# Attention with relative positions on one core: the order in which sixteen products of the relative-value table are issued

## The chip, the core and the metric

The kernel runs on one core of a Trainium2 chip. The core has a matrix engine (TensorE, called PE in the profile, with its weight loads shown apart as PEld), VectorE (DVE), ScalarE (ACT), GpSimd (POOL) and SyncE (SP), each with its own instruction stream; they meet in semaphores. TensorE writes into PSUM, which has eight banks here. TensorE's array is used in four column groups of 32 columns: a product whose result goes to PSUM partitions 32q to 32q+31 runs in column group q. The metric is the device time of one execution, in microseconds.

## The reference

Four sequences of 1024 tokens with 128 channels are normalised, and two branches are added to the input: attention with 16 heads of 8 channels, and a routed feed-forward part (64 experts, six of them for each token, and a shared one). The change lies in the attention, in the term of the output that comes from the table of relative values:

```python
rp = _rp_bucket(N)          # clip(j - i, -31, 31) + 31, 63 buckets
attn = softmax(q k + qL + kL)
out = jnp.einsum('bhij,bhjd->bhid', attn, v)
S = segment_sum(attn over j, by rp)         # per query i and bucket n
out = out + jnp.einsum('inbh,hnd->bhid', S, rpe_v_table)
```

## The kernel before, in words

A unit of work is a head of one batch; there are 4 x 16 = 64 of them, called heads below. For each head the 1024 x 1024 scores are computed twice: once for the maxima (result in banks 0 and 1, reduced by VectorE, line 1408, tile `tops`), and once with the maximum folded in (banks 2 and 3, exponentiated by ScalarE, line 1096, into the tile `PT`). Each pass has 16 units of half a bank row, and the loop of every engine is written in 16 slots `s` of one iteration. In an iteration TensorE does pass one of head h+1, pass two of head h (six slots behind), and parts of other heads between. The order on each engine is the order of the code; there is no scheduler.

What stands around the change, in TensorE's order: at slot 11 the two products for the table of a later head go to banks 6 and 7 (`dq_psum`); ScalarE copies them to `dq_e` (line 1115); SyncE writes them to memory (`dq_d`, line 544) and reads them back skewed (`dq_s`, line 483); at slot 5 of the next iteration TensorE transposes `dq_s` (line 944). At slot 13 stands the function `near`: GpSimd has copied a window of `PT` around the diagonal to `WP` (line 638), the head's relative values lie in `TOE` as a band matrix, and 48 small products of the two add up in bank 6. VectorE masks them into `Ym` (line 1454), and at slot 15 four products put them on the head's output (`rel_done`). Then follow the `values` products (`PT` with `Vst`, tile names `PS<-PT,Vst`), the last score units, and at slot 1 of the next iteration the transposition of the maxima (`top`, line 914), which waits for VectorE (line 1404). When `near` is done, SyncE reloads `TOE` for every other head (line 478).

`near` is one list of 48 products (b, k). The group is q = ((b - 8) mod 32) // 8. All products are in float32, and each is recorded as two weight loads and two matmuls, so that the trace has 96 matmuls per head. The first 32 products are 32 columns wide, the other 16, which take the neighbouring row block (k = -1 or 1), are 28 wide. Line 697 is a helper through which nearly all matmuls go; in the trace the products of `near` are the rows with `PS<-WP,TOE`.

TensorE's stream is filled up with small semaphore instructions (`pause`) so that an iteration has 1024 instructions. After 30 heads the loop is left for the experts (about 777 to 866 us), then it goes on.

Of the kernel before, what the change touches and what calls it, by code (L numbers as in the profile page):

```python
# [86 lines left out]
def program(nc, x, wqkvg, w_proj, b_proj, rk_far, rq_far, rk_dist, rq_dist, rv_rows, rv_far,  # L87
# [19 lines left out]
    with ctx:  # L107
# [587 lines left out]
        def _(pe):  # L695
            def mm(o, l, r, start=True, stop=True):
                return pe.matmul(o, l, r, start=start, stop=stop, skip_group_check=True)  # L697
# [158 lines left out]

            def near(h):

                for b, k in [(8 + 8 * q + a, 0) for a in range(8) for q in range(4)] + [(b, -1) for b in range(8)] + [(b, 1) for b in range(40, 48)]:
                    to = (b - 8) % 32  # L860
                    q, a = to // 8, to % 8
                    J0, J1 = max(0, -k), min(NJ, NJ - k)
                    ins = mm(PS[TILE * q:TILE * q + TILE, 6, 32 * a + 4 * (J0 + k):32 * a + 4 * (J1 + k)],
                             TOE[:, SPAN - 4 * b - 4:SPAN - 4 * b, :].rearrange("p a b -> p (a b)"), WP[:, J0:J1, 4 * b:4 * b + 4],
                             start=k == 0 and a == 0)
                ins.then_inc(y_psum, 1)
# [26 lines left out]
            def iteration(i, c, peeled):  # L893
# [3 lines left out]
                for s in range(SLOTS):  # L897
# [54 lines left out]
                    if s == 13 and on(-1):  # L952

                        misc_free(h, (top_read, h + 1), (on_ready, h - 1), (aj_copied, h + 4, 2), (dq_copied, h + 5))
                        pe.wait_ge(toe_in, 16 * sum(fresh(k) for k in range(h)))
                        for part in range(2):
                            pe.wait_ge(win_in[part], h)
                        near(h - 1)
# [52 lines left out]
            for e in range(QUADS):  # L1011
                p, k = e % 2, e % SETS
# [8 lines left out]
                for m in range(4):  # L1021
                    half, a = m // 2, m % 2
# [561 lines left out]
```

## Time and profile before

| | us |
|---|---|
| median of three runs | 1529.62 |
| lowest and highest run | 1525.92, 1534.31 |
| span of the profiled execution, first to last instruction | 1522.0 |
| TensorE busy (matmuls) | 1325.6 (87%) |
| VectorE busy | 1111.2 (73%) |
| ScalarE busy | 797.9 (52%) |
| GpSimd busy | 541.3 (36%) |

Of the profiled execution the profile gives the span, from the first instruction to the last; its whole time, with what lies around the span, is not given apart. The median of the runs is 7.6 us above the span. In the profile a row gives a group of instructions by line and engine, the tiles that they write and read (`out<-in`), their shapes, their count, the time in which at least one of them ran, the mean duration of one in ns, and the idle time of the engine just before them with what ended it. "issue" there is a wait for nothing that the profile shows. The granted clock of TensorE is the share of its full speed.

### The profile page before, as it was taken

What the parts mean: (1) busy time and instruction counts of PE and PEld (TensorE: products, weight loads), DVE (VectorE), ACT (ScalarE), POOL (GpSimd) and SP (SyncE); (2) the same over time, 40 slices, a digit from 0 to 9 for tenths busy, and PEclk for the clock granted to TensorE, in tenths of its full rate; (3) what the DMA queues carried; (4) which work ended last, traced back from release to release, by engine and by line L of the source; (5) the groups of instructions that cost most, each with busy time, mean ns of one, the idle gap of its engine ahead of it and who ended that gap; (6) DMA issues with size and microseconds to landing.
All of it is one profiled execution on the core that took longest, in us unless ns stands there. A gap on an engine that the chain in (4) does not pass through costs nothing. (4 is left out here: it accounts for less than half of the span.)

```text
span 1522.0 us, 75140 instructions
## 1 busy us (share of the span) xinstructions
PE 1325.6 (87%) x32698; PEld 895.9 (59%) x32698; DVE 1111.2 (73%) x2461; ACT 797.9 (52%) x1408; POOL 541.3 (36%) x552
## 2 busy tenths in 40 slices
PE   2785399999999999988989899999999999999887
PEld 1352256666666666655668565666666666666555
DVE  7684378888888888887764676777777767777762
ACT  1332135655665666655541455665666555656544
POOL 3453212222222222222434244444444444444423
PEclk9897559999999999999995799999999999999999
DMA  4444546666556555554564566666666666666532
GB/s 97 138 142 138 159 158 200 200 207 193 186 183 191 190 176 183 181 184 153 174 189 145 160 183 182 183 192 198 186 183 196 183 176 180 190 183 183 149 104 58
DMA packets 167209, 260.10 MB, mean 171 GB/s; under 512 B 33980, under 2 KB 89397, under 8 KB 166886
## 3 DMA queue, kind: packets, MB, share of 16 engines
q1 hardware_dynamic: 155414, 248.46, 52.5%
q0 software_dynamic: 11472, 6.83, 3.7%
q8 instruction: 264, 4.33, 1.1%
q14 instruction: 59, 0.48, 0.1%
HBM read 145.14 MB, written 112.37 MB: 169 GB/s over the span
## 5 line engine op out<-in xcount | busy, mean ns | idle before, releaser
L1408 DVE TRANSPOSE_TENSOR_REDUCE tops<-PS 128x16 f32<-128x512 f32 x1024 | 689.7, 699 | 190.1 <-PE PS L697 183.9
L1096 ACT ACTIVATE PT<-PS 128x512 f32<-128x512 f32 x1024 | 590.2, 596 | 423.4 <-PE PS L697 416.1
L697 PE MATMUL PS<-Qs,Ks 73*32 73x512 bf16 (+29 forms) x11904 | 666.4, 322 | 66.8 <-DVE tops L1408 45.6
L697 PEld LDWEIGHTS PS<-Qs,Ks 73*32 73x32 bf16 (+1 forms) x11904 | 308.9, 97 | 266.7 <-DVE tops L1408 94.0
L697 PE MATMUL PS<-PT,Vst 128*9 128x256 f32 (+7 forms) x7552 | 345.4, 286 | 12.6 <-issue 12.1
L638 POOL COPY WP<-PT 128x768 f32<-128x768 f32 x128 | 105.3, 822 | 645.4 <-ACT PT L1096 460.9
L697 PE MATMUL PS<-WT,eye 96*32 96x96 bf16 (+2 forms) x4352 | 294.7, 206 | 0.2 <-issue 0.2
L697 PEld LDWEIGHTS PS<-PT,Vst 128*9 128x9 f32 x7552 | 187.8, 91 | 82.6 <-issue 32.3
L697 PEld LDWEIGHTS PS<-WT,eye 96*32 96x32 bf16 x4352 | 186.8, 99 | 22.5 <-issue 1.2
L657 POOL TENSOR_TENSOR ajp<-dq_s,ajp 128x508 bf16<-128x508 f32 x128 | 147.3, 1151 | 10.4
L626 POOL DMA_INDIRECT acc_d<-XNA,tok_i x64 | 100.8, 1575 | 78.8 <-DMA acc_d<-XNA,tok_i 66.2
L1120 ACT ACTIVATE ajp<-PS 128x508 bf16<-128x508 f32 x128 | 76.8, 600 | 95.4 <-PE PS L697 95.4
L655 POOL CAST ajp<-dq_s 128x508 bf16<-128x508 f32 x128 | 78.7, 615 | 125.2 <-DVE dq_s L1449 125.2
L944 PE MATMUL PS<-ident,dq_s 127*128 127x127 f32 x512 | 86.5, 295 | 39.5 <-DMA dq_s<-dq_d 39.3
L697 PE MATMUL PS<-WP,TOE 128*32 128x32 f32 x6144 | 110.1, 197 | 5.4 <-issue 4.7
L697 PEld LDWEIGHTS PS<-WP,TOE 128*32 128x32 f32 x6144 | 103.8, 111 | 18.3 <-issue 17.4
L1449 DVE TENSOR_TENSOR dq_s<-PS,ajp 128x508 f32<-128x508 f32 x128 | 83.2, 650 | 27.9 <-ACT ajp L1120 27.9
L1115 ACT ACTIVATE dq_e<-PS 128x1024 f32<-128x1024 f32 x64 | 65.6, 1024 | 41.7 <-PE PS L697 41.7
L944 PEld LDWEIGHTS PS<-ident,dq_s 127*128 127x128 f32 x512 | 58.4, 151 | 46.9 <-issue 44.2
L1454 DVE TENSOR_TENSOR Ym<-PS,ymask 128x256 f32<-128x256 f32 x64 | 27.2, 425 | 75.6 <-PE PS L697 75.6
L697 PE MATMUL PS<-PT,WT 128*88 128x512 f32 (+2 forms) x128 | 56.0, 632 | 18.5 <-DVE Ym L1290 6.2
L697 PE MATMUL PS<-tab,Ks 79*128 79x127 bf16 x512 | 53.6, 231 | 0.0
(199 smaller groups left out, 1025.9 us busy)
## 6 DMA issues: line engine op xcount, KB each, us to landing
aj_d<-ajp SPq DMA_DIRECT2D x64, 768.0 KB
WT<-aj_d SPq DMA_DIRECT2D x192, 256.0 KB
dq_d<-dq_e SPq DMA_DIRECT2D x64, 512.0 KB, 5.3
dq_s<-dq_d SPq DMA_DIRECT2D x64, 512.0 KB, 3.9
TOE<-toe_d SPq DMA_DIRECT2D x33, 768.0 KB, 5.8
q_stack<-PT SPq DMA_DIRECT2D x24, 256.0 KB, 2.5
Qs<-q_stack SPq DMA_DIRECT2D x64, 96.0 KB
Ks<-k_stack SPq DMA_DIRECT2D x64, 96.0 KB
```

What stands on the lines that cost most here:

```text
L626: pool.indirect_dma_start(out=acc_d, out_offset=bass.IndirectOffsetOnAxis(ap=tok_i[:, 1 + half, n:n + 1], axis=0), in_=Y[:, n, :], in_offs ...
L638: pool.tensor_copy(WP[:, 4 * part:4 * part + 4, :], src).then_inc(win_in[part], 1)
L655: pool.tensor_copy(low[:, 0], r1).then_inc(aj_mid, 1)
L657: pool.tensor_tensor(low[:, 1], r1, low[:, 0], ALU.subtract).then_inc(aj_parts, 1)
L697: return pe.matmul(o, l, r, start=start, stop=stop, skip_group_check=True)
L944: pe.matmul(PS[:, bank, a * P:a * P + DIST], dq_s[0:DIST, J * P:(J + 1) * P], ident[0:DIST, 0:DIST], start=a == 0, stop=False, is_transpos ...
L1096: act.activation(PT[:, TILE + N * J + 512 * half:TILE + N * J + 512 * half + 512], PS[:, 2 + u % 2, :], ACT.Exp).then_inc(s2_read, 1)
L1115: act.activation(dq_e[:, :], MISC, ACT.Copy).then_inc(dq_copied, 1)
L1120: act.activation(ajp[:, 0, 4 * part:4 * part + 4, 0:DIST], PS[:, 6 + part, :].rearrange("p (a n) -> p a n", n=P)[:, :, 0:DIST], ACT.Copy). ...
L1408: dve.tensor_reduce(tops[:, (h + 1) % 2, s // 2, 16 * (s % 2):16 * (s % 2) + 16], PS[:, s % 2, :].rearrange("p (c i) -> p c i", i=TILE), A ...
L1449: dve.tensor_tensor(dst, src, ajp[:, 0, 4 * part:4 * part + 4, 0:DIST], ALU.subtract).then_inc(aj_copied, 1)
L1454: dve.tensor_tensor(Ym[:, :].rearrange("p (t a x) -> p a t x", t=NJ, x=4), PS[:, 6, 0:256].rearrange("p (a t x) -> p a t x", t=NJ, x=4), y ...
```

## The change

The same 48 products are issued, with the same operands and results. Before, the four groups take turns over the first 32 products, and then come the eight products of b = 0 to 7, all in group 3, and the eight of b = 40 to 47, all in group 0. Now each group has its own list, the lists are taken in turns to the end, and in the last 16 products group 0 and group 3 alternate: (40, 1), (0, -1), (41, 1), (1, -1) and so on to (47, 1), (7, -1).

```diff
             def near(h):
 
-                for b, k in [(8 + 8 * q + a, 0) for a in range(8) for q in range(4)] + [(b, -1) for b in range(8)] + [(b, 1) for b in range(40, 48)]:
+                own = [[(8 + 8 * q + a, 0) for a in range(8)] for q in range(4)]
+                own[0] += [(b, 1) for b in range(40, 48)]
+                own[3] += [(b, -1) for b in range(8)]
+                for b, k in (mine[n] for n in range(16) for mine in own if n < len(mine)):
                     to = (b - 8) % 32
                     q, a = to // 8, to % 8
```

TensorE's stream before, from the end of the score unit of slot 13 to the `values` products behind `near` (one row is a run of products of one shape, with the partitions and columns of the result):

```order
L697 MATMUL PS<-Qs,Ks 32x512 x4
L697 MATMUL PS<-WT,eye3 32x32
L697 MATMUL PS<-WP,TOE 32x32 x32
L697 MATMUL PS<-WP,TOE 32x28 x16
L697 MATMUL PS<-PT,Vst 9x64 x3
L697 MATMUL PS<-PT,Vst 9x32
```

The same place of TensorE's stream in the changed kernel:

```order
L697 MATMUL PS<-Qs,Ks 32x512 x4
L697 MATMUL PS<-WT,eye3 32x32
L697 MATMUL PS<-WP,TOE 32x32 x32
L697 MATMUL PS<-WP,TOE 32x28 x16
L697 MATMUL PS<-PT,Vst 9x64 x3
L697 MATMUL PS<-PT,Vst 9x32
```

The rows read alike, since they do not show the column group: what moved stands inside the one row of sixteen 28-wide products, where eight of group 3 and then eight of group 0 became pairs of one of each. The product that signals `y_psum` is now one of group 3, (7, -1); before it was (47, 1) of group 0. No other engine's stream differs.

## Rows read from the trace of the kernel before

**Rows 1.** The page: engines, then VectorE's costliest group and `near`

```profile
PE 1325.6 (87%) x32698; PEld 895.9 (59%) x32698; DVE 1111.2 (73%) x2461; ACT 797.9 (52%) x1408; POOL 541.3 (36%) x552
...
L1408 DVE TRANSPOSE_TENSOR_REDUCE tops<-PS 128x16 f32<-128x512 f32 x1024 | 689.7, 699 | 190.1 <-PE PS L697 183.9
...
L697 PE MATMUL PS<-WP,TOE 128*32 128x32 f32 x6144 | 110.1, 197 | 5.4 <-issue 4.7
```

**Rows 2.** The engines' busy time by stretch: us, busy, clock, DMA share, GB/s

```profile
238.70:777.50 538.80, 494.95 (x13937) 334.37 (x13932) 455.62 (x1024) 322.47 (x569) 150.72 (x176) 1.00 0.59 186
866.30:1437.40 571.10, 531.71 (x14912) 364.98 (x14911) 422.81 (x870) 341.14 (x600) 246.60 (x241) 0.99 0.65 184
```

**Rows 3.** Groups of TensorE by shape, 1094.86 to 1096.53 us, one `near`

```profile
L697 PE MATMUL PS<-WP,TOE 128*32 128x28 f32 x32 | 1.1, 193 | 0.0
L697 PE MATMUL PS<-WP,TOE 128*32 128x32 f32 x64 | 0.8, 198 | 0.0
```

**Rows 4.** TensorE's timeline at the end of `near`: start, us, work

```profile
700.55 1.25 PE L697 MATMUL PS<-WP,TOE 128*32 128x32 f32 x83
702.21 0.53 PE L697 MATMUL PS<-WP,TOE 128*32 128x28 f32 x12 [0.40 <-issue]
...
1094.86 1.63 PE L697 MATMUL PS<-WP,TOE 128*32 128x32 f32 x95
1096.30 0.23 PE L697 MATMUL PS<-PT,Vst 128*9 128x64 f32 x3
```

**Rows 5.** VectorE's timeline behind a `near`: start, us, work, idle before

```profile
505.91 0.42 DVE L1454 TENSOR_TENSOR Ym<-PS,ymask 128x256 f32<-128x256 f32 x1 [0.43 <-PE PS L697]
506.67 1.37 DVE L1408 TRANSPOSE_TENSOR_REDUCE tops<-PS 128x16 f32<-128x512 f32 x2 [0.34 <-PE PS L697]
```

**Rows 6.** Who waited for whom, 238 to 777 us: us, times, longest

```profile
DVE Ym L1454 <- PE PS L697: 22.3, 28, 2.0
...
PE PS L944 <- DMA dq_s<-dq_d: 5.6, 4, 2.0
```

**Rows 7.** The same, 866 to 1430 us

```profile
PE PS L944 <- DMA dq_s<-dq_d: 12.3, 13, 1.8
...
PEld PS L697 <- issue: 45.5, 154, 2.2
```

**Rows 8.** The chain that ended last, one head: start, us, what

```profile
1092.95 1.03 ACT dq_e L1115
1094.00 5.76 DMA dq_d<-dq_e
1099.78 4.58 DMA dq_s<-dq_d
```

**Rows 9.** Timelines around TensorE's use of `dq_s`

```profile
1104.66 0.62 PE L944 MATMUL PS<-ident,dq_s 127*128 127x127 f32 x4 [0.69 <-DMA dq_s<-dq_d]
...
1006.56 0.33 SPq L483 DMA_DIRECT2D dq_s<-dq_d  x1
...
1010.74 0.33 PE L944 MATMUL PS<-ident,dq_s 127*128 127x127 f32 x1
```

**Rows 10.** DMA issues, us to landing last: that transfer, and `TOE` (page)

```profile
dq_s<-dq_d SPq DMA_DIRECT2D x1, 512.0 KB, 3.5
...
TOE<-toe_d SPq DMA_DIRECT2D x33, 768.0 KB, 5.8
```

**Rows 11.** TensorE's timeline in the `values` behind `near`, two heads

```profile
1120.14 0.50 PE L697 MATMUL PS<-PT,Vst 128*9 128x128 f32 x11 [0.53 <-issue]
...
1311.15 0.50 PE L697 MATMUL PS<-PT,Vst 128*9 128x128 f32 x11 [0.26 <-issue]
```

**Rows 12.** DMA queues of the page: packets, MB, share of 16 engines

```profile
q8 instruction: 264, 4.33, 1.1%
```

**Rows 13.** TensorE's waits, 1437 to 1522 us

```profile
PE PS L697 <- issue: 7.2, 6, 3.6
```

**Rows 14.** DMA and throughput of one `near`, 1094.85 to 1095.45 us: PE busy, clock, DMA share

```profile
1094.85:1095.45 0.60, 0.60 (x70) 1.00 0.95 358
```

## The prediction

> **What bounds the kernel now.** I read the page first, then the busy time by stretch, then the waits of each half of the head loop, and last the timelines of single heads. The page shows TensorE busy 87% of the span and VectorE 73%; the reductions of the maxima are VectorE's largest item, 1024 x 699 ns, and the products that the change reorders are 6144 records with 110.1 us of busy time, 1.72 us for each of the 64 heads [rows 1]. The two halves of the loop, on either side of the experts, last 538.8 and 571.1 us, and TensorE is busy 92% and 93% of them, at the full clock (1.00 and 0.99) [rows 2]. So TensorE sets the pace, but not alone: three things interrupt it, and the question is what a shorter `near` meets.
>
> First, VectorE. In a head of the first half VectorE idles 0.43 us before `Ym`, waiting for the end of `near`, and 0.34 us again for the score unit behind it [rows 5]; over the first half that wait is 22.3 us in 28 heads, 0.8 us each [rows 6]. VectorE then works on what `near` has released. A shorter `near` therefore starts VectorE's part earlier too, as long as the cut is no more than the smallest of these idle times, about 0.43 us.
>
> Second, the round trip of `dq` through memory. It starts at slot 11, before `near`, and ends at slot 5 of the next iteration: 1.03 us on ScalarE, 5.76 us out, 4.58 us back [rows 8]. In that head TensorE stood 0.69 us before the transposition [rows 9]. This happens 4 times in the first half and 13 times in the second [rows 6, 7]. `near` lies between the start and the end of this trip but is no part of it.
>
> Third, "issue" waits, in which TensorE waits for nothing that the profile shows. One of them stands inside `near`, always behind the 82nd or 83rd of the 96 records: 0.40 us of idle time in the head at 700.55 us, none in the head at 1094.86 [rows 4]. I read it as instructions that come late: the queue of instruction packets moved 264 packets [rows 12], and TensorE recorded 32698 matmuls and as many loads [rows 1], 248 for each packet, about a quarter of an iteration of 1024 instructions; since every iteration has the same number, the edge of a packet falls on the same place in every head. Stepping through the 64 groups in the timeline, 20 have a gap there (12 in the first half). The next edge is in the `values` products some 4.4 us later; in the second half nearly every head stands there, for 0.26 or 0.53 us [rows 11], part of 45.5 us of issue waits of the weight loads [rows 7].
>
> **The change, part by part.** It adds and removes no instruction, no wait and no DMA, and moves work in TensorE's stream only. In an undisturbed head the 64 records that are 32 wide, issued with four groups in turn, are busy 0.8 us together, and the 32 records that are 28 wide 1.1 us [rows 3]. The whole lasts 1.63 us for 95 of the 96 [rows 4]. Taking the last record's own 0.19 us off 1.1 leaves 0.9 us for 32 starts: the two runs of one group each start a record every 32 ns with a slight overlap where group 3 hands over to group 0 (16 x 32 ns twice would be 1.02 us). In the first part the starts come every 0.6 us / 64 = 9 ns, which is some 35 ns within one group. So a group takes a record every 32 to 35 ns, and groups overlap. With two groups in turn the 32 records take 16 x 32 ns = 0.51 us. Cut per head: 0.89 - 0.51 = **0.38 us**. Bounds: nothing, if two groups side by side went no faster than one, and 0.89 - 32 x 9 ns = 0.60 us, if the pace of four groups held; I take 0.38, since the pace within one group is in the row and two groups cannot beat twice that. 64 x 0.38 = 24.3 us is the most that the mechanism gives if all of it reaches the end. The `values` products behind `near` start 0.03 us before its last record now [rows 4], so nothing more is hidden or uncovered there.
>
> A rule of the Trainium skill speaks against this: "TensorE: Matmul & The Clock Gate", section "Wait — 56ns, not 53.3ns?", has it that starts of matmuls never come closer than about 25 ns, however few columns. By it the 32 records would still take 32 x 25 ns = 0.8 us and the cut would be about 0.1 us per head, 6 us at most in all. The trace disagrees: 64 records with a mean of 198 ns in 0.8 us are 9 ns apart [rows 3].
>
> Now what of the 24.3 us arrives.
>
> First half, 29 heads. In 4 the transposition waits for `dq_s` [rows 6], and the last runs into the experts, whose own start waits for other things: 5 heads x 0. In 12 the instructions are late inside `near`. The edge does not come earlier, and only the 14 records behind it gain, 14 x 16 ns = 0.2 us: 12 x 0.2 = 2.4 us. In the remaining 12 TensorE now gets to the edge 0.19 us earlier (half the cut lies before it), and where instructions were just in time a small new wait arises; I take 0.05 us off: 12 x 0.33 = 4.0 us. VectorE's idle time of 0.43 us or more covers the cut. Sum 6.4 us.
>
> Second half, 30 heads. 13 wait for `dq_s` [rows 7], and in four more the transfer lands within 0.1 us of its use: 17 x 0. The other heads have room: at 1006.56 us the transfer is issued and lands 3.5 us later, at 1010.06, while TensorE transposes at 1010.74 [rows 9, 10]; where it waits, it starts 0.3 us after the landing (1099.78 + 4.58 = 1104.36, start 1104.66 [rows 8, 9]). Slack 0.68 - 0.3 = 0.4 us, just enough for 0.38. But these heads stand at the next edge, 0.26 or 0.53 us [rows 11], and I do not expect those instructions to come earlier, because the DMA engines are full during `near` (share 0.95 [rows 14]) and the fetch stands in their queues. Behind that wait TensorE today catches up with VectorE's maxima, so part of it is covered. Bounds for such a head 0 and 0.38 us; I take the middle, 0.2: 13 x 0.2 = 2.6 us.
>
> The last 5 heads have no `dq` any more, but 7.2 us of issue waits in six places [rows 13]. Two of five at 0.38 give 0.8 us.
>
> Sum: 6.4 + 2.6 + 0.8 = 9.8 us. Against the execution's own span, 1522.0 - 9.8 = 1512.2 us; what lies around the span stays, so against the median of the runs, 7.6 us above, 1529.6 - 9.8 = **1519.8 us**, in round numbers 1520.
>
> A smaller effect: every other head reloads `TOE` (768 KB [rows 10]) when `near` is done, now 0.38 us earlier. The engines are full then, and the reload only changes its place in a queue that is busy anyway; cost or gain is bounded by 0.38 us in the 17 heads that are bound by the transfer, 6.5 us to either side, and I take nothing.
>
> **Rivals.**
>
> All of it arrives. For it: TensorE busy above 92% in both halves [rows 2], and VectorE idle before `Ym` [rows 6]. Against it: the 17 heads whose transposition comes with the transfer. 1529.6 - 24.3 = 1505 us.
>
> Nothing measurable arrives. The instruction fetch and the transfer take it all: the fetch holds TensorE at the edge inside `near` or at the next one, and the time won is spent there. For it: 45.5 us of issue waits in the second half [rows 7], and the slack of 0.4 us is no more than the cut. Against it: in the first half there is no wait at the next edge in nearly all heads. 1529.6 - 0 to 5: 1525 to 1530 us.
>
> The two groups do not run side by side as four do, say because the two passes of one float32 product stand next to each other and hold the other group back. Then the pace is between 32 and 16 ns, half the cut arises, and half of 9.8 is left: 1525 us. Against it: the same pairs stand in the first 32 products, and those run at 9 ns.
>
> Slower: late instructions are noticed in steps. The waits in rows 11 are 0.26 and 0.53 us, one and two of the same step. If TensorE gets to the next edge 0.38 us earlier while the packet lands when it did, it waits 0.38 us rounded up to two steps, 0.53 us, and loses 0.15 us per head. This decides if the edge is on the path in most heads, as it is in the second half and not in the first. 64 x 0.15 = 9.6 us: 1539 us.
>
> **How the numbers follow.** Forecast 0.58, all of it 0.10, nothing measurable 0.19, half the overlap 0.05, slower 0.08. A measurement of this kernel can tell 0.5% from no change, 7.6 us here. The forecast's own range is 1514 to 1525, and four fifths of it are beyond 7.6 us (0.46); with all of the second and a little of the others faster comes to 0.58, slower is the last case with 0.08, and 0.34 is left for no change. The range 1509 to 1530 leaves out the full gain and the slower case beyond its start, together under 2 in 10.
>
> **What would show it.** `near` itself: 32 records 28 wide with busy time 0.7 us instead of 1.1, and about 1.25 us from its first start to the end of its last record, in all undisturbed heads; if it stays at 1.63 the overlap is wrong. The group's busy time on the page should fall from 110.1 to about 86 us. VectorE's wait before `Ym` should fall in the first half from 0.8 to about 0.5 us a head. The waits of the transposition for `dq_s` should rise in number (above 17 over both halves) and by about 0.38 us each in the bound heads; if they do not rise, more arrives than I say. The issue waits in `near` and in the `values` should rise; if they rise by more than the cut, the slower case has come.

## The result

The changed kernel takes 1561.94 us (median of four runs, 1557.12 to 1568.82) against 1527.77 us for the kernel before on the same chip: ratio 1.0245, 95% interval 1.0188 to 1.0301. It is 2.4% slower, and the time lies outside the range that was given. Here and below a ratio leaves out executions that were disturbed and clearly slower than the others of the same kernel, so it can differ by some tenths of a per cent from the quotient of the two medians.

The page of the changed kernel: span and engines, the queue that carries TensorE's instruction packets (`q8`), and then the groups that answer to [rows 1], with the one that took the time.

```profile
span 1555.3 us, 75140 instructions
...
PE 1311.4 (84%) x32698; PEld 890.6 (57%) x32698; DVE 1119.9 (72%) x2461; ACT 798.4 (51%) x1408; POOL 541.3 (35%) x552
...
q8 instruction: 264, 4.33, 1.2%
...
L697 PE MATMUL PS<-PT,Vst 128*9 128x256 f32 (+7 forms) x7552 | 369.6, 290 | 56.5 <-issue 55.2
...
L697 PE MATMUL PS<-WP,TOE 128*32 128x32 f32 (+1 forms) x6144 | 89.7, 197 | 15.0 <-issue 14.1
```

The row of `near` did what was said: its busy time fell from 110.1 [rows 1] to 89.7 us, 0.32 us a head. But TensorE's idle time before it rose from 5.4 to 15.0 us, and before the `values` products, which stood in the page of before as

```profile
L697 PE MATMUL PS<-PT,Vst 128*9 128x256 f32 (+7 forms) x7552 | 345.4, 286 | 12.6 <-issue 12.1
```

it rose from 12.6 to 56.5 us, nearly all of it "issue". In sum -20.4 + 9.6 + 43.9 = 33.1 us is about the difference of the spans, 1555.3 - 1522.0 = 33.3. Other rows changed too (the `values` products were busy 24 us longer, the waits for `dq_s` fell by 12 us), so this is no complete account, but it says where to look.

The same stretches as in [rows 2], in the changed kernel (us, busy time of PE, PEld, DVE, ACT, POOL, clock, DMA share, GB/s):

```profile
237.50:781.70 544.20, 481.75 (x13441) 330.18 (x13438) 445.40 (x995) 311.78 (x549) 143.76 (x168) 0.97 0.57 177
886.60:1469.20 582.60, 527.25 (x14913) 363.43 (x14912) 427.29 (x870) 341.46 (x600) 246.69 (x241) 0.98 0.64 181
```

The second holds the same 30 heads as the second of [rows 2], and takes 582.6 us instead of 571.1. The first holds one head less (it starts its 28th `near` at 781.7 us), so it counts 27 heads in 544.2 us, where 28 took 538.8.

One undisturbed `near` in the changed kernel, by shape, as [rows 3]:

```profile
L697 PE MATMUL PS<-WP,TOE 128*32 128x32 f32 x64 | 0.8, 198 | 0.0
L697 PE MATMUL PS<-WP,TOE 128*32 128x28 f32 x32 | 0.7, 193 | 0.0
```

The 28-wide records are busy 0.7 us instead of 1.1: the two groups do run side by side, at 16 ns a record (0.51 us from the first start to the last, 31 steps).

Now the place that costs. TensorE's timeline of a head in which `TOE` is reloaded, in the changed kernel (start, us, work, idle before):

```profile
379.06 1.31 PE L697 MATMUL PS<-WP,TOE 128*32 128x32 f32 x92
...
384.12 0.29 PE L917 MATMUL PS<-ident,top 128*32 128x128 f32 x1 [0.29 <-DVE top L1407]
384.61 0.38 PE L697 MATMUL PS<-PT,Vst 128*9 128x128 f32 x3
386.40 0.50 PE L697 MATMUL PS<-PT,Vst 128*9 128x128 f32 x11 [1.40 <-issue]
```

and of such a head in the kernel before:

```profile
294.70 1.63 PE L697 MATMUL PS<-WP,TOE 128*32 128x32 f32 x95
...
300.02 0.28 PE L914 MATMUL PS<-ident,top 128*32 128x128 f32 x1 [0.39 <-DVE top L1404]
300.51 0.61 PE L697 MATMUL PS<-PT,Vst 128*9 128x128 f32 x16
```

The wait stands at the 202nd record behind the start of `near`, where the next instruction packet begins, 120 records after the edge inside `near`. Below, a long wait is a step of over 1 us from the start of one record to the start of the next; such a step holds TensorE's idle time and about 0.2 us of the record before it. Stepping through the timeline, there is a long wait at this place in all 29 heads that reload `TOE` between the first and the 59th (idle time alone 0.80 to 2.31 us), and in none of the 29 that do not; before there were two. Head after head, the time from one `near` to the next is, on average (us):

| | before | changed |
|---|---|---|
| first half, 14 heads without reload | 19.03 | 18.98 |
| first half, 14 heads with reload | 19.46 | 21.45 |
| second half, 15 heads without reload | 18.89 | 18.39 |
| second half, 15 heads with reload | 19.18 | 20.44 |

So the whole loss lies in the heads with a reload: 14 x 2.0 + 15 x 1.3 = 47 us, against 8 us gained in the others, and the rest around the experts (the one head that holds them is 5.8 us shorter, with 31 instead of 65 us of it at the lower clock).

The 47 us are not waits alone. In 14 of the 29 reload heads the granted clock fell to 0.5, the lower of its two levels, for 3.4 or 6.8 us: in ten within 2 us behind a stop at this place, in two during it, and in two behind another stop of TensorE. In the 29 heads without reload it never fell, and in the kernel before it fell in two reload heads and one other. One such head, the end of the stop in TensorE's timeline and the stretch behind it (us, busy time of PE, PEld, DVE, ACT, POOL, clock, DMA share, GB/s):

```profile
424.75 0.50 PE L697 MATMUL PS<-PT,Vst 128*9 128x128 f32 x11 [2.04 <-issue]
...
425.15:428.56 3.41, 3.41 (x71) 3.29 (x65) 1.43 (x2) 1.19 (x2) 0.00 (x0) 0.50 0.05 7
```

Summed over the 29 reload heads, TensorE was idle 35 us longer than before and busy 11.5 us longer, although its part for `near` was about 9 us shorter. They spent 55 instead of 7 us at the lower clock; if work takes twice as long there, that is 24 us, an estimate from these two figures, and it fits the busy time. So the waits start the loss, and about two fifths of it are paid at the lower clock behind them.

The DMA queues say what happens at the stop. In the changed kernel, from just before SyncE issues the reload to 3.6 us later (packets, MB, share of 16 engines), no packet of `q8` moves, only one of the smaller packets of `q14`, which carried 59 packets of 8 KB in the whole execution; with 1.1 us more in the window, a packet of `q8` does:

```profile
q1 hardware_dynamic: 292, 1.30, 101.5%
q14 instruction: 1, 0.01, 2.5%
TOE<-toe_d SPq DMA_DIRECT2D x1, 768.0 KB
...
q1 hardware_dynamic: 356, 1.55, 94.3%
q14 instruction: 1, 0.01, 1.9%
q8 instruction: 1, 0.02, 1.2%
```

In the kernel before, a window of 4 us from just before the end of `near` (296.0 to 300.0 us, the reload is issued at 296.39) already has the packet:

```profile
q8 instruction: 1, 0.02, 1.5%
...
TOE<-toe_d SPq DMA_DIRECT2D x1, 768.0 KB, 4.8
```

### The profile page after: what moved, and what is told of

Its sections match the earlier page's. It is cut to its first block and busy times, and to the rows that moved or that the text cites. A ratio compares the mean times of both kernels' runs of the same rounds, so it can differ in the third digit from the quotient of the medians.

```text
span 1555.3 us, 75140 instructions
## 1 busy us (share of the span) xinstructions
PE 1311.4 (84%) x32698; PEld 890.6 (57%) x32698; DVE 1119.9 (72%) x2461; ACT 798.4 (51%) x1408; POOL 541.3 (35%) x552
## 3 DMA queue, kind: packets, MB, share of 16 engines
q8 instruction: 264, 4.33, 1.2%
## 5 line engine op out<-in xcount | busy, mean ns | idle before, releaser
L697 PE MATMUL PS<-Qs,Ks 73*32 73x512 bf16 (+29 forms) x11904 | 688.7, 327 | 66.6 <-DVE tops L1411 36.7
L697 PEld LDWEIGHTS PS<-Qs,Ks 73*32 73x32 bf16 (+1 forms) x11904 | 342.2, 99 | 251.1 <-DVE tops L1411 73.0
L697 PE MATMUL PS<-PT,Vst 128*9 128x256 f32 (+7 forms) x7552 | 369.6, 290 | 56.5 <-issue 55.2
L697 PE MATMUL PS<-WT,eye 96*32 96x96 bf16 (+2 forms) x4352 | 319.3, 208 | 1.0 <-issue 1.0
L697 PEld LDWEIGHTS PS<-PT,Vst 128*9 128x9 f32 x7552 | 201.0, 92 | 131.9 <-issue 81.6
L697 PEld LDWEIGHTS PS<-WT,eye 96*32 96x32 bf16 x4352 | 204.8, 100 | 23.4 <-issue 2.6
L657 POOL TENSOR_TENSOR ajp<-dq_s,ajp 128x508 bf16<-128x508 f32 x128 | 147.4, 1151 | 10.4
L697 PE MATMUL PS<-WP,TOE 128*32 128x32 f32 (+1 forms) x6144 | 89.7, 197 | 15.0 <-issue 14.1
L697 PEld LDWEIGHTS PS<-WP,TOE 128*32 128x32 f32 x6144 | 80.3, 111 | 31.1 <-issue 29.3
```

The source lines that it names most:

```text
L657: pool.tensor_tensor(low[:, 1], r1, low[:, 0], ALU.subtract).then_inc(aj_parts, 1)
```

## The experiments

Two theories stood. A, order of arrival: TensorE asks for the next packet when it crosses an edge. `near` contains an edge at record 82, and its end releases the reload of `TOE`. Between the two lay 0.63 us before and 0.47 us now (from the start of record 82 to that of the last 0.24 instead of 0.41 us). With the shorter lead the 768 KB of the reload get to the DMA engines first and the packet comes late. B, pace: TensorE reaches the edges sooner than instructions come, whatever the reload does.

**Release the reload later.** The changed kernel with

```diff
-                    wait(sp, y_psum, h - 1)
+                    wait(sp, ym_ready, h - 1)
                     own = toe_d[...]
```

> The changed kernel, with the reload of TOE released by VectorE's Ym (0.65 us later) instead of by the end of near. Theory A (order of arrival): the change cut the time between TensorE's crossing of the packet edge in near, which asks for the next instructions, and the issue of the reload of TOE from 0.63 to 0.47 us, so that in every other head the 768 KB reload is served first and the instructions come 1.4 to 2.3 us late. Then this kernel loses those waits: the step before record 202 in the reload heads falls from 1.4 to 2.0 us on average to 0.6 us or less, and the time is 1510 to 1530 us. Rival B (pace): TensorE simply reaches both edges sooner than instructions can be supplied, whatever the reload does: nothing changes, 1555 to 1568 us.

Measured 1540.92 us, before 1536.43 on that chip, ratio 1.0017 (0.9987 to 1.0046). The loss is gone, with nothing changed on TensorE. The time is above the stated range in microseconds, but the kernel before was 9 us slower here too; as a ratio it is just above the range too (1530 us against 1527.77 is 1.0015). The idle time before the `values` products fell from 56.5 to 32.5 us:

```profile
L697 PE MATMUL PS<-PT,Vst 128*9 128x256 f32 (+7 forms) x7552 | 358.5, 287 | 32.5 <-issue 31.2
```

15 of the 29 reload heads still had a long wait, and the step averaged 1.0 to 1.1 us instead of 0.6 or less: the later reload is not out of the way in all heads.

**Move the edge later in the kernel before.** Its order untouched:

```diff
-START = 58
+START = 44
```

> The kernel before, its order of products untouched, with 44 instead of 58 pause instructions at the start of TensorE's stream, so that the packet edge falls some seven records later inside near (record 89 of 96) and the time between crossing it and the reload of TOE shrinks from 0.63 to about 0.41 us. Theory A: as slow as the changed kernel, 1550 to 1570 us, with waits of 1.4 to 2.3 us about 120 records behind the edge in the reload heads. Rival B: TensorE's pace between edges is as before and the edge comes 0.2 us later, so nothing or a small gain, 1520 to 1532 us.

Measured 1564.65 us, ratio 1.0228 (1.0146 to 1.0309): as slow as the change within the intervals, without the change (by the medians alone 1.018, from four executions). This is the strongest evidence that the order of the products does not cost anything itself; what costs is the shorter time between the edge and the reload. The time went where A says: first-half heads with reload took 21.15 us instead of 19.46, those without 19.09 instead of 19.03. But there were 9 and 4 long waits in the 14 and 15 reload heads of the two halves, fewer than A asked for: in the second half a lead of 0.41 us mostly did no harm, and a reload head took 19.39 us there instead of 19.18.

**No reloads, with both orders.** `TOE` is loaded only for head 0 and behind the experts; the kernel leaves out the reload of the other heads, whose relative-value term is then that of an old table.

```diff
-            return h % 2 == 0 or h == hm - 1
+            return h == 0 or h == hm - 1
```

> The changed kernel with TOE loaded only for head 0 and after the experts (the relative-value term of the other heads is left wrong), so the reloads every other head are gone. Theory A: the long waits for instructions are gone and the cut of 0.38 us in near shows: 5 to 15 us below the kernel before with the same edit, at 1495 to 1515 us. Rival B: 20 us or more above the kernel before with the same edit. A third possibility C, that the earlier reload hurts by delaying dq_s, would also give a time like theory A, but then the waits that vanish are those for dq_s and not the issue waits.

> The kernel before with TOE loaded only for head 0 and after the experts (the relative-value term of the other heads is left wrong): the base for the run above. Theory A: 1505 to 1525 us, since the transfer of dq_s no longer stands behind the reload in every other head. Rival B: the same; this run is there to measure the change of order without reloads.

Measured 1524.53 us (ratio to before 0.9908, 0.9871 to 0.9945) and 1524.22 us (0.9916, 0.9873 to 0.9959). Rival B falls for this change: without the reload the changed order costs nothing, and its long waits went from 29 to 2. But A's own number fell too: the order gains nothing either. `near` is shorter by the same amount, and TensorE waits for instructions instead. `near` with the changed order and with the old one, both without reload:

```profile
L697 PE MATMUL PS<-WP,TOE 128*32 128x32 f32 (+1 forms) x6144 | 90.9, 197 | 24.3 <-issue 24.0
```

```profile
L697 PE MATMUL PS<-WP,TOE 128*32 128x32 f32 x6144 | 114.6, 197 | 13.9 <-issue 13.4
```

23.7 us less busy, 10.4 us more idle there; over all rows of line 697 the issue waits are 50.7 and 32.5 us:

```profile
PE PS L697 <- issue: 50.7, 87, 7.4
```

```profile
PE PS L697 <- issue: 32.5, 39, 7.6
```

18 of the 24 us have become issue waits.

**Move the edge earlier.** 84 pauses at the start, edge at record 69:

```diff
-START = 58
+START = 84
```

> The changed kernel with 84 instead of 58 pause instructions at the start of TensorE's stream: the packet edge falls 13 records earlier in near (record 69), and the time from crossing it to the issue of the TOE reload grows from 0.47 to about 0.7 us, without touching the reload. Theory A (order of arrival of the instruction packet and the reload) expects the waits of more than 1 us behind the next edge (now record 189) to go from 29 reload heads of 29 to fewer than 5, and the time to 1510 to 1530 us. Rival B (pace alone) expects the same waits at the new places: 1550 to 1565 us. Under A, if the smaller waits inside near also shrink, because the dense products are now shared between two packets, it ends below the kernel before; if it ends level with it, the supply of instructions keeps the cut.

> The kernel before with the same 84 pause instructions, edge at record 69 of near: the control for the run above. Theory A: the lead over the reload grows from 0.63 to 1.0 us, nothing to lose, 1518 to 1532 us. Rival B: the same. If the changed order has any worth of its own, the changed kernel with this edge is 5 to 15 us below this one; if the supply of instructions keeps the cut, they are level.

Measured 1535.36 us (ratio 1.0014, 0.9974 to 1.0054) for the changed order and 1542.79 us (1.0045, 1.0015 to 1.0076) for the old one, before 1536.43. The change with this edge is 2.3% faster against the kernel before than it was with its own: a second way to remove the loss, this time without touching the reload. The long waits are 10 of 29 instead of the "fewer than 5" expected. The changed order is 7 us below the old one by the medians, inside the 5 to 15 us that stood for a worth of its own, but the two intervals overlap. The steps at the edge inside `near` did not shrink, they grew (for the changed kernel from averages of 0.3 to 0.5 us, by half and kind of head, to 0.4 to 0.65 us).

**Reload behind the reading of `dq_s`.** The two blocks of SyncE's iteration exchanged, with 84 pauses.

```diff
             def iteration(i, c, peeled):
-                if on(-1) and fresh(h - 1):
-                    wait(sp, y_psum, h - 1)
-                    ...
                 if on(3):
                     sp.wait_ge(dq_out, 16 * (h + 4))
                     ...
+                if on(-1) and fresh(h - 1):
+                    wait(sp, y_psum, h - 1)
+                    ...
```

> The changed kernel with the edge at record 69 and, in SyncE's order, the reload of TOE behind the reading of dq_s instead of ahead of it. Theory A: the reload now starts some 4.5 us after near, far behind both the instruction packet and dq_s, so both the long issue waits and the 17 waits for dq_s in every other head go: 1500 to 1515 us, the fastest. Rival B: level with the changed kernel, 1550 to 1565 us. Against both: the reload may then stand ahead of the small transfers of the maxima (Qs from mparts), which TensorE's second pass waits for; then 1520 to 1535 us.

Measured 1568.01 us, ratio 1.0215 (1.0158 to 1.0272): a miss. The waits for `dq_s` did go, from 7.7 us with 84 pauses alone to 0.5 us between 238 and 1440 us. The caveat named one new place: the reload now stands ahead of the three small transfers of the maxima. In the chain that ended last such a transfer takes 5 us:

```profile
529.58 5.54 DMA Qs<-mparts
...
651.65 5.25 DMA Qs<-mparts
...
693.05 5.02 DMA Qs<-mparts
```

where their median is 1.8 us in the kernel before; 20 of the 192 took over 4 us here, and one there. The caveat's size was too small. It is not the whole cost: TensorE's issue waits also rose, from 43.4 to 72.2 us in the same stretch, and why they did was not followed up.

**Both: edge early and reload late.**

> The changed kernel with the edge at record 69 and the reload of TOE released by VectorE's Ym. Theory A: with this edge the lead is already long enough, so the later release adds little: within 0.5% of the changed kernel with the early edge alone. If it is faster by 1% or more, the lead of 0.7 us was still too short. Rival B: 1550 to 1565 us.

> The kernel before with 84 pauses (edge at record 69 of near) and the reload of TOE released by VectorE's Ym: the control for the changed kernel with both edits, which stood at 0.996 of the kernel before. If the changed order is worth something where the reload is out of the way, this one is 0.5 to 1.5% slower than that, at 1.000 to 1.010 of the kernel before. If supply keeps the whole cut, it is level with it, 0.992 to 1.000.

Measured 1531.49 us for the changed order (ratio 0.996, 0.9925 to 0.9994) and, on another chip, 1528.93 us for the old one (1.0018, 0.9984 to 1.0051). The first is the only kernel of this study, apart from those that leave work out, whose interval lies wholly below 1, and by a hair (by the medians alone 0.997). The ratios differ by 0.6%, some 9 us, with intervals that overlap a little: with the reload out of the way the order may be worth what the prediction said, but this is not shown.

**Two more placements.** Only the late release, on the kernel before; and the changed kernel with the late release and 70 pauses.

> The kernel before with only the reload of TOE released by Ym. Theory A: its lead of 0.63 us was enough, so no gain in the first half, and the reload now stands 0.65 us later against dq_s: 0.997 to 1.012 of the kernel before. If order of arrival had cost the kernel before something in its second half too (waits of 0.65 us in the reload heads there), it is 0.985 to 0.995.

> The changed kernel with the reload released by Ym and 70 pauses: edge at record 76 of near, between the two places tried (82 with 1.0017, 69 with 0.996). Theory A: 0.993 to 1.002 of the kernel before. Against it: where the packet falls among the other transfers weighs more than the lead, and it may be anywhere up to 1.02.

Measured 1521.62 us (0.9974, 0.9946 to 1.0002) and 1524.59 us (0.9986, 0.9954 to 1.0018), before 1525.49. Both level with the kernel before. That gives a pair with the late release and 58 pauses too, 1.0017 with the changed order and 0.9974 with the old one, on two chips: here the changed order is 0.4% behind. Of the pairs of equal edits with a time near the kernel's own, two lean to the changed order (0.3% and 0.6%), this one against it, and the one without reloads to neither side.

**How much the place of the edge weighs.** 214, 130 and 30 pauses instead of 58.

> The changed kernel with 214 pause instructions at the start: the packet edge stands at record 4 of near, so that near lies whole in one packet, and the edge is crossed some 1.3 us before the reload of TOE is issued. Theory A has two parts: the order of arrival (lead over the reload) and the supply (a packet is asked for when the one before is entered, and comes no sooner than 3.3 us later, crossing to start of fetch 1.1, transfer 0.95, landing to use 1.25). The lead is safe, so few waits over 1.5 us in reload heads; but near's packet now runs for under 3 us, so the next edge (record 124) waits in every head, reload or not, and 1535 to 1555 us. Rival B (pace alone, no part for the reload) expects 1550 to 1570, the same in heads with and without reload.

> The kernel before with the same 214 pauses: the control. Supply part of theory A: its near is 0.38 us longer and its wait at record 124 that much shorter, so it is level with the changed kernel at the same edge, within 0.7%. If supply does not hold the cut, the changed kernel is 10 to 20 us faster than this one.

> The changed kernel with 130 pauses, edge at record 46 of near, the middle: the dense products are shared by two packets and the lead over the reload is 1.0 us. Theory A: no long waits in reload heads, and the smaller ones least of all: 1515 to 1535 us. If the waits at the edge are set by what else is in the DMA queues then (dq_d and ajp going out) and not by the time between edges, it is no better than the edge at record 69: 1530 to 1545 us. Rival B: 1550 us or more.

> The changed kernel with 30 pauses, edge at record 96, behind the last of near's records: the lead over the reload is 0.25 us. Theory A: the long waits behind the next edge (record 216) in nearly all reload heads, as in the changed kernel, 1555 to 1575 us. Rival B: the packet after the edge has no record of near and takes 4 us or more, so the waits there go, 1520 to 1540 us.

Measured, before 1544.65 on that chip: 1784.9 us (ratio 1.1572) with the changed order and the edge at record 4, 1785.94 us (1.1598) with the old order there; 1704.33 us (1.1073) in the middle; 1665.27 us (1.072) at the end (no line of its profile is used here against the others). The sizes of all four were missed by far. What held is the comparison: the two orders are level to 0.3% where `near` lies whole in one packet, though `near` itself is 25 us shorter:

```profile
L697 PE MATMUL PS<-WP,TOE 128*32 128x32 f32 (+1 forms) x6144 | 85.9, 198 | 3.2 <-issue 3.2
...
PE PS L697 <- issue: 180.8, 81, 7.4
```

```profile
L697 PE MATMUL PS<-WP,TOE 128*32 128x32 f32 x6144 | 110.5, 197 | 4.5 <-issue 4.5
...
PE PS L697 <- issue: 161.4, 82, 7.4
```

19 of the 25 us are again issue waits. Which share of the 240 us is waiting and which is what the waits set off was not taken apart; the granted clock fell too, to 0.849 on average with the changed order, from 0.937 in the kernel before. Here the order of arrival is not the cause: with 214 pauses and the changed order, long waits 120 records behind the edge stand in 24 of the 29 reload heads and in 27 of the 29 others, though the lead is 1.26 us. Where the edge lies badly, TensorE waits for packets with or without a reload, which is what rival B describes.

## Why the prediction was wrong, point by point

**What bounds the kernel.** The three things that a shorter `near` meets were named rightly, with the packet edge at its place. (VectorE's smallest idle time in rows 5 is 0.34 us, for the score unit behind, not 0.43; and the stop at the next edge stands in 16 of the 30 heads of the second half with 0.2 us or more of idle time, not in nearly all.) What was wrong is the order of their weight: I counted the packets as something that would take part of the gain in the second half, when they decide the sign.

**The size of the cut** was right: 0.38 us said, 0.32 us a head in the busy time of the whole group (20.4 / 64), and 0.4 us in the 28-wide records of an undisturbed head. Expected was "about 86 us", measured 89.7. The rival of an incomplete overlap, and with it the 25 ns of the Trainium skill's page on TensorE ("TensorE: Matmul & The Clock Gate", section "Wait — 56ns, not 53.3ns?"), is out: 32 records in 0.7 us less the last one's 0.19 are 16 ns apart.

**"VectorE's idle time of 0.43 us or more covers the cut"** is not contradicted: VectorE's wait before `Ym` fell from 22.3 to 18.7 us between 238 and 777 us, less than from 0.8 to 0.5 us a head as was said, and the period of the heads without reload did not grow. No run tests it alone.

**The waits for `dq_s`** were expected to rise above 17. They fell. TensorE now comes later to them, which is the likely reason:

```profile
PE PS L947 <- DMA dq_s<-dq_d: 3.6, 2, 1.8
...
PE PS L947 <- DMA dq_s<-dq_d: 1.8, 3, 1.0
```

(238 to 777 us, and 887 to 1467), 5 instead of 4 and 13 [rows 6, 7]. A wait that vanishes was here the sign of a worse one ahead of it.

**The step that failed** is the "smaller effect" at the end of the sum: "every other head reloads `TOE` (768 KB) when `near` is done, now 0.38 us earlier. The engines are full then, and the reload only changes its place in a queue that is busy anyway". I bounded it by 0.38 us a head, the shift itself, and took nothing. But two requests stand 0.63 us apart there, the instruction packet and the reload, and a shift that lets the large one pass the small one costs the small one up to the large one's time. That is about 2.2 us for 768 KB at the 358 GB/s of [rows 14], an estimate; the packet started 2.5 us later in the first half. With the lower clock behind the stop, a reload head lost 2.0 us in the first half and 1.3 in the second. I had both in hand, the edge at record 82 and the release of the reload by the last record, and did not set their times side by side. The experiments show this step: with the order unchanged and the lead cut to 0.41 us the loss is there (1.0228), and with the order changed it goes when the reload is released later (1.0017) or the edge comes earlier (1.0014). The prediction had no term at all for the clock, which stood at 1.00 and 0.99 in the rows that it read.

**The gain of 9.8 us** did not come either, and this is a second step, a term that was mis-sized. In the first-half heads without reload I took 0.05 us off the cut of 0.38 for a new wait at the edge inside `near`; the step there grew by 0.27 us on average, from 0.15 to 0.42, and a head became 0.05 us shorter instead of 0.33. In the second half a head without reload became 0.5 us shorter, more than the 0.2 that I gave to 13 of 30. Without reloads the two orders end level, and 18 of the 24 us won in `near` come back as issue waits.

**The slower rival** had the right place, the packet edge behind `near`, and the right sign, with a chance of 0.08; its price was 0.15 us a head, since it let the packet land when it did before. It starts later by about 2.5 us in a reload head of the first half: from crossing the edge to the start of the packet's transfer the median is 1.7 us before and 4.2 us now, and 4.2 us also in the kernel before with the edge moved to record 89. In the second half it is 2.7 us before and 3.7 now.

**"Nothing measurable arrives"** turned out true of what is left once the reload is out: without reloads both orders take the same time.

What stays open: the lead alone does not explain every head. With 0.41 us the second half was mostly spared, with 0.9 us 15 of 29 heads still waited. What else is in the queues at that moment plays a part that was not taken apart. With the edge at record 46 and a lead of 0.9 us, long waits stand in 24 of 29 reload heads. And why the placements at records 4 to 46 cost 11 to 16% was not followed up. No experiment holds the clock apart from the waits. When TensorE asks for a packet the trace does not show, only when its transfer starts: in the kernel before 1.0 us after the crossing at the earliest. That it is asked for at the crossing is an assumption of theory A.

## What to carry to other kernels

In a kernel whose instruction stream is thick (here 75140 instructions in 1.5 ms), instructions are traffic beside the kernel's own transfers: an "issue" wait that comes back at the same record of every iteration is probably the edge of a packet (it moves when instructions are added or taken away ahead of the loop), and a faster stretch changes both when the next packet is asked for and what is queued ahead of it. Before making a stretch shorter, list what its end releases and what its middle requests, with the time between them: where a large transfer is 0.5 us from overtaking a small one that an engine waits for, the price can be the large one's length, not the shift, and the clock may fall behind the wait. Then move the edge or the release along with the change, and try the same move on the old kernel.

## What was not expected of the hardware

The place of a packet's edge within the loop was worth far more than the change: 156 more semaphore instructions at the very start of TensorE's stream, outside any loop, made the kernel 16% slower (1785.94 with the old order against 1544.65 us), with either order of products, and 14 fewer made it 2.3% slower. In the first half an instruction packet of 16 KB started 2.5 us later than before behind the reload, while the engines moved 292 other packets in 3.7 us. And behind or during stops of 1.4 to 2.3 us the granted clock fell to 0.5 for 3.4 us or more in 14 of the 58 heads, which added some 24 us (the estimate above) to 35 us of idle time; behind other stops as long it did not fall. The Trainium skill ("Runtime: NRT & Kernel Launch", section "Instruction fetch mechanics") gives the same frame, blocks of 16 KiB or 256 instructions that the sequencer fetches while it runs the one before, and the trace agrees with the size (264 packets of 4.33 MB together); but it calls the cost of crossing an edge mostly hidden, since instructions are issued more slowly than they are fetched. The kernel before roughly agrees: its issue waits were 29.3 us, 0.1 us for each of the 264 packets. The changed kernel, with 90.9 us, and the one with the edge at record 4, with 180.8 us, do not:

```profile
PE PS L697 <- issue: 90.9, 112, 7.4
```

```profile
PE PS L697 <- issue: 29.3, 33, 7.6
```
